# Relation passes of a graph network: messages and mixed rows worked on in PSUM, rings of four, squares of shares made by ScalarE

## The chip, the cores and the metric

The kernel runs on one core of a Trainium2 chip. The metric is the device time of one execution in microseconds. The names of the engines in the profile: PE is TensorE (PEld its weight loads), DVE is VectorE, ACT is ScalarE, POOL is GpSimd, SP is SyncE, which here only issues DMAs.

## The reference

Four graph layers run one after the other on x, 50000 nodes of 128 float32 values: a graph attention network, a relation network, a GraphSAGE network and an equivariant network, each added to x and normalized. The change touches only the relation network. It takes its input x as h, with 25000 edges (src, dst, type), dst sorted, and runs three cells:

```python
def _cell(h_in, relv, W, b, src, dst, rel, n_nodes):
    msg = jax.nn.relu(h_in[src] + relv[rel])
    s = jax.ops.segment_sum(msg, dst, num_segments=n_nodes)
    cnt = jax.ops.segment_sum(jnp.ones((src.shape[0],), msg.dtype), dst, num_segments=n_nodes)
    red = s / jnp.maximum(cnt, 1.0)[:, None]
    return red @ W.T + b
h = _cell(h, relvecs[0], lin_w[0], lin_b[0], ...)
for l in range(1, N_LAYERS):
    h_prev = h
    _h = jax.nn.relu(_layer_norm(h, ln_w[l - 1], ln_b[l - 1]))
    h = h_prev + _cell(_h, relvecs[l], lin_w[l], lin_b[l], ...)
h = _layer_norm(h, ln_w[-1], ln_b[-1])
```

After it, x becomes the layer norm of x + h. Only nodes with incoming edges differ from a closed form, so the kernel works on "slots", one per edge position in sorted order: 49 blocks of 512 slots (128 partitions, KT = 4 columns).

## The kernel before, in words

The program is a row of passes, each closed by a barrier of all engines. The three relation passes are `RelSlots(l)` for l = 0, 1, 2 (from 2728 us of the span to 3737). Before them lie the attention passes, behind them three sage passes (`SageSlots`) and the last pass `tp`.

Each engine runs its own list of steps through `times` (L136): a step has a lag, and at time t a step with lag d works on block t - d; the order inside the list is the order of issue within one time. Waits are on semaphores that count blocks: `done(engine, sem, b, back)` waits until block b - back has passed `sem`, `landed` waits for a DMA.

For one block b, in passes 0 and 1:

- GpSimd (L1687) issues four indirect DMAs, each of which fetches 128 rows of the sources into `G` (ring of 4). It waits for the messages of block g - 4. The descriptors of these DMAs are made on GpSimd itself.
- TensorE `messages` (L1702): one matmul adds the relation vectors (`relv` by a one-hot `oh`) into the bank `pt`, then four matmuls multiply each 128 gathered rows by a diagonal square with the shares (1 / count) of their slots, `kn.shares`. The result is turned: features on partitions, slots along the free dimension.
- ScalarE `relu` (L1741) writes it to SBUF as `mT` (ring of 2).
- VectorE `run_sums` (`run_scan`, L1603) scans along the slots with the 0/1 marks `kn.same`, which gives the segment sums `agT` (SBUF).
- TensorE `product` (L1715) multiplies by the weights into the bank `pw` (ring of 2).
- VectorE `mix` (L1794) adds the bias or the row of the cell before (`prev`) and writes `y` in SBUF. `next_bias` (L1805) adds the next bias for the store `yb`.
- ScalarE `square` (L1746) and `deviation` make the row norms' deviation. VectorE `scale` takes the reciprocal, `norm` (L1815) writes y * r * weight to `u` (SBUF), `cut` (L1822) does the relu against the negative bias. SP stores `yb` and `u`.

In pass 0 VectorE also makes the diagonal squares with the shares for all later passes (`spread_shares`, L1789: one 128x512 product of the identity with four columns of `shareD` spread out, both in SBUF).

Pass 2 has, in place of `next_bias`, `norm` and `cut`, the steps of `end_steps` (L1062): `gamma` (four scalings of y), `add_x` (adds the node's x, loaded to `xx`), `stats`, `aggregate`, `scale2`, `shift` on VectorE, `norm` on ScalarE (four activations to `nrm`). Then TensorE `turn` transposes `nrm` into the bank `pn` (L1724), ScalarE `keep_turned` (L1763) copies it to `nT` (ring of 2), SP stores it to `sage_slots_t` with lag 11 (L1671), TensorE `rows` multiplies it into the bank `pr` (L1729), ScalarE `keep_rows` (L1770) copies it to `res` (ring of 2), and SP stores that. `keep_turned` waits until the store of the block two before has landed.

Of the kernel before, what the change touches and what calls it, by code (L numbers as in the profile page):

```python
# [1608 lines left out]
class RelSlots(Stream):  # L1609


    def __init__(self, kn, q, l):
        self.kn, self.l, self.last = kn, l, l == 2
        self.G = q.sb("G", [P, 4, KT, D])
        self.Y = 2 if self.last else 4
        self.oh = q.sb("oh", [8, self.Y, BLOCK])
        self.mT = q.sb("mT", [P, 2, BLOCK])
        self.agT = q.sb("agT", [P, self.Y, BLOCK])
        self.y = q.sb("y", [P, self.Y, KT, D])
        self.yb = q.sb("yb", [P, 4, KT, D]) if l < 2 else None  # L1620
        self.prev = q.sb("prev", [P, 4, KT, D]) if l else None
        self.junk = q.sb("junk", [P, KT, D])
        self.ss, self.sd, self.rr = (q.sb(n, [P, 4, KT]) for n in ("ss", "sd", "rr"))
        self.pt = [q.ps(f"t{j}") for j in range(2)]
        self.pw = [q.ps(f"w{j}") for j in range(2)]
        self.gin, self.ohin, self.pin = (q.sems(n, 4) for n in ("rows_in", "kinds_in", "before_in"))
        if l < 2:
            self.stored, self.ystored = q.sems("stored", 4), q.sems("y_stored", 4)
        (self.mtm, self.mtk, self.scn, self.wm, self.shd, self.yn, self.ym, self.sq, self.sdm, self.rrd) = (
            q.sem(n) for n in ("messages_made", "messages_kept", "summed", "product_made", "shares_ready", "next_bias_added", "mixed",  # L1630
                               "squares_made", "deviation_ready", "scale_ready"))
        if self.last:
# [3 lines left out]
            self.e = kn.end_steps(self.parts, lambda b, k: self.y[:, b.m % self.Y, k, :], self.rr, self.ym, self.rrd, lambda n: kn.slot_at(kn.n0, kn.NP, n), None,  # L1636
                                  kn.lw[:, 2, :])
            self.nT = q.sb("nT", [P, 2, BLOCK])
            self.res = q.sb("res", [P, 2, KT, D])
            self.pn, self.pr = q.ps("nt"), q.ps("r")  # L1640
            self.tstored, self.rstored = q.sems("turned_stored", 4), q.sems("rows_stored", 4)
            self.gate, self.xb, self.ntr, self.ntk, self.rm, self.rk = (
                q.sem(n) for n in ("store_gate", "x_beta", "out_turned", "out_kept", "rows_made", "rows_kept"))
        else:
            self.u = q.sb("u", [P, 4, KT, D])
            self.un, self.um = q.sem("normed"), q.sem("result_ready")

    def sync(self, sp):
# [50 lines left out]
    def tensor(self, pe):  # L1699
        kn, l = self.kn, self.l  # L1700

        def messages(b):  # L1702
            landed(pe, self.ohin, b)
            landed(pe, self.gin, b, 0, 16 * KT)
            done(pe, self.mtk, b, 2)
            if l == 0:
                done(pe, self.shd, b)
            pt = self.pt[b.s2]
# [6 lines left out]
        def product(b):  # L1715
            done(pe, self.scn, b)
            done(pe, self.ym, b, 2)
            for k in range(KT):
                mm = pe.matmul(self.pw[b.s2][:, k * P:(k + 1) * P], self.agT[:, b.m % self.Y, k * P:(k + 1) * P], kn.Wr[:, l, :], start=True, stop=True)
            mm.then_inc(self.wm, 1)  # L1720
# [8 lines left out]
        def rows(b):  # L1729
            done(pe, self.ntk, b)  # L1730
            done(pe, self.rk, b, 1)
            for k in range(KT):
                mm = pe.matmul(self.pr[:, k * P:(k + 1) * P], self.nT[:, b.s2, k * P:(k + 1) * P], kn.Wn[:, 0, :], start=True, stop=True)
# [4 lines left out]
    def scalar(self, act):  # L1738
        kn, l = self.kn, self.l

        def relu(b):  # L1741
            done(act, self.mtm, b)
            done(act, self.scn, b, 2)
            act.activation(self.mT[:, b.s2, :], self.pt[b.s2][:, :], ACT.Relu).then_inc(self.mtk, 1)  # L1744

        def square(b):  # L1746
# [3 lines left out]
            for k in range(KT):  # L1750
                last = act.activation(self.junk[:, k, :], self.y[:, b.m % self.Y, k, :], ACT.Square, scale=D ** -0.5, accum_out=self.ss[:, b.s4, k:k + 1])
# [11 lines left out]
        def keep_turned(b):  # L1763
            done(act, self.ntr, b)
            done(act, self.rm, b, 2)
            if not isinstance(b.n, int) or b.n >= 2:
                act.wait_ge(self.tstored[(b.m + 2) % 4], (b.i + (b.m - 2) // 4 + 1) * 16)
            act.activation(self.nT[:, b.s2, :], self.pn[:, :], ACT.Copy).then_inc(self.ntk, 1)

        def keep_rows(b):  # L1770
            done(act, self.rm, b)
            if not isinstance(b.n, int) or b.n >= 2:
                act.wait_ge(self.rstored[(b.m + 2) % 4], (b.i + (b.m - 2) // 4 + 1) * 16)
            act.activation(self.res[:, b.s2].rearrange("p k d -> p (k d)"), self.pr[:, :], ACT.Copy).then_inc(self.rk, 1)
# [3 lines left out]
        return [(deviation, 5), (square, 4), (relu, 1)]  # L1778

    def vector(self, v):  # L1780
        kn, l = self.kn, self.l

        def run_sums(b):
# [55 lines left out]
        return ([] if l else [(spread_shares, 0)]) + [(cut, 6), (mix, 4), (run_sums, 2), (next_bias, 4), (scale, 5), (norm, 5)]  # L1839
# [1273 lines left out]
```

## Time and profile before

| | us |
|---|---|
| median of 3 runs | 5241.16 (5229.94 to 5247.69) |
| the profiled execution's own time | 5236.16 |
| its span | 5234.4 |
| PE / DVE / ACT / POOL busy | 3823.6 / 3793.3 / 3176.2 / 2889.9 |
| TensorE's granted clock, mean | 0.85 |
| relation pass 0, 1, 2 | 2728 to 3047, to 3348, to 3737 |

The busy time of an engine is an average over passes with different limits, so the rows of one pass say more than the table. A granted clock of 1.0 is 2.4 GHz and 0.5 is 1.2 GHz; a mean in between is a mix of the two. "Idle before" of a group is the time its engine waited just before its instructions, with what ended the wait; "issue" is idle time that ends with nothing the profile shows.

### The profile page before, as it was taken

Reading aid. Unit: us, or ns where it says so; the run is one execution under the profiler, and the core shown is the slowest. Engines: PE = TensorE matmul, PEld = TensorE weight load, DVE = VectorE, ACT = ScalarE, POOL = GpSimd, SP = SyncE. Lnnn points to the kernel's source line nnn. Section 1 sums busy time; section 2 is a strip of 40 time slices with the busy share of each in tenths; the row PEclk is TensorE's granted clock in tenths of the full one; section 3 lists DMA queues with packets and bytes.
Section 4 is the critical chain, followed back from the end, with each engine's and each line's share of the span. In section 5 each row is a group of like instructions: output and inputs, shape, how many; then the busy total and the mean of one; then the engine's idle time right before and its main releaser. Section 6 shows DMA issues by size and latency. Waiting matters only on the chain. (4 is left out here: it accounts for less than half of the span.)

```text
span 5234.4 us, 104308 instructions
## 1 busy us (share of the span) xinstructions
PE 3823.6 (73%) x23663; PEld 3147.4 (60%) x23663; DVE 3793.3 (72%) x10843; ACT 3176.2 (61%) x11279; POOL 2889.9 (55%) x2759
## 2 busy tenths in 40 slices
PE   6355889876877676577767767677688887967775
PEld 5254778765557455555655545466576676856665
DVE  1575889987869787887977767677577675746665
ACT  2022879786868687787753323366687685645554
POOL 0474767604730770175017767666374765757776
PEclk8698999988989898899766666688899998978777
DMA  8899999756965885598653446455598896772221
GB/s 183 117 295 276 378 371 294 248 149 188 286 202 155 238 280 170 158 281 263 169 165 119 131 147 188 153 180 185 187 307 284 271 305 224 245 173 58 64 67 55
DMA packets 918272, 1074.23 MB, mean 205 GB/s; under 512 B 202779, under 2 KB 565065, under 8 KB 917106
## 3 DMA queue, kind: packets, MB, share of 16 engines
q1 hardware_dynamic: 763570, 890.24, 52.2%
q0 software_dynamic: 90944, 180.06, 14.2%
q10 hardware_dynamic: 63556, 1.81, 1.7%
q14 instruction: 146, 1.20, 0.1%
q8 instruction: 56, 0.92, 0.1%
HBM read 509.54 MB, written 566.14 MB: 206 GB/s over the span
## 5 line engine op out<-in xcount | busy, mean ns | idle before, releaser
L2359 POOL DMA_INDIRECT H<-gat_rows,src_i x784 | 803.2, 1024 | 879.8 <-POOLq L80 641.8
L1910 POOL DMA_INDIRECT s_G<-sage_rows,src_i x588 | 604.1, 1027 | 363.5 <-issue 162.5
L1696 POOL DMA_INDIRECT r_G<-rel_rows,idx x392 | 438.4, 1118 | 207.9 <-issue 111.9
L2548 PE MATMUL p_M<-Wg,p_hT 128*128 128x132 f32 x2352 | 337.8, 287 | 64.2 <-DVE p_res L2605 49.5
L1709 PE MATMUL r_t<-r_oh,relv 8*128 8x512 f32 x294 | 227.1, 861 | 207.9 <-issue 94.6
L1744 ACT ACTIVATE r_mT<-r_t 128x512 f32<-128x512 f32 x147 | 87.3, 594 | 457.4 <-PE r_t L1712 457.3
L2548 PEld LDWEIGHTS p_M<-Wg,p_hT 128*128 128x128 f32 x2352 | 290.9, 192 | 115.2 <-issue 98.2
L2605 DVE SCALAR_TENSOR_TENSOR p_res<-p_M,p_rr,cg 128x132 f32<-128x132 f32 x1176 | 334.0, 346 | 2.3 <-PE p_M L2548 1.4
L1305 PE MATMUL d_S<-ones,d_sqT 128*128 128x1 f32 x1568 | 228.6, 267 | 135.9 <-DVE d_ve L1450 135.9
L2687 PEld LDWEIGHTS p_pl_p<-Wn,p_pl_h 128*128 128x128 f32 x1568 | 204.2, 197 | 205.3 <-ACT p_pl_h L2781 156.3
L2687 PE MATMUL p_pl_p<-Wn,p_pl_h 128*128 128x128 f32 x1568 | 223.7, 288 | 136.1 <-ACT p_pl_h L2781 134.2
L1305 PEld LDWEIGHTS d_S<-ones,d_sqT 128*128 128x128 f32 x1568 | 222.0, 218 | 162.7 <-issue 131.7
L1606 DVE TENSOR_TENSOR_SCAN r_agT<-same_run,r_agT,r_mT 128x512 f32<-128x512 f32 (+1 forms) x144 | 184.5, 1281 | 179.7 <-ACT r_mT L1744 179.7
L1712 PEld LDWEIGHTS r_t<-share_squares,r_G 128*128 128x128 f32 x1176 | 198.9, 256 | 159.5 <-issue 159.5
L1696 POOL DMA_INDIRECT r_G<-n_rows,src_i x196 | 235.8, 1203 | 78.5 <-issue 55.5
L2407 POOL DMA_INDIRECT H<-gat_rows,dst_i x196 | 196.1, 1001 | 141.1 <-POOLq L80 59.2
L2120 POOL DMA_INDIRECT share_squares<-features,src_i x196 | 217.1, 1108 | 93.0 <-issue 59.2
L964 POOL DMA_INDIRECT gat_rows<-early_mapv,early_mput x196 | 193.9, 989 | 122.7 <-PEq L77 59.6
L1354 ACT ACTIVATE d_hs<-d_hs,pl 128x128 f32<-128x128 f32 x784 | 248.3, 398 | 15.4 <-DMA d_hs<-gat_rows 11.6
L1444 DVE TENSOR_TENSOR_SCAN d_yT<-same_run,d_yT,d_T 128x512 f32<-128x512 f32 (+1 forms) x192 | 244.4, 1273 | 0.5 <-PE d_T L1298 0.4
L2112 POOL DMA_INDIRECT out_dram<-tp_v,put_i x196 | 198.1, 1011 | 78.8 <-issue 57.0
L1712 PE MATMUL r_t<-share_squares,r_G 128*128 (+1 forms) x1176 | 234.5, 361 | 0.0
(482 smaller groups left out, 12290.6 us busy)
## 6 DMA issues: line engine op xcount, KB each, us to landing
gat_rows<-p_res SPq DMA_DIRECT2D x294, 264.0 KB
sage_rows<-p_pl_s SPq DMA_DIRECT2D x294, 256.0 KB
gat_rows<-x_row SPq DMA_DIRECT2D x98, 536.0 KB
gat_rows<-d_res SPq DMA_DIRECT2D x147, 264.0 KB
d_hs<-gat_rows SPq DMA_DIRECT2D x147, 256.0 KB
s_hT<-sage_slots_t SPq DMA_DIRECT2D x147, 256.0 KB
slot_rows<-H SPq DMA_DIRECT2D x49, 544.0 KB, 11.3
x_x<-in_x SPq DMA_DIRECT2D x98, 256.0 KB
```

The source lines that it names most:

```text
L1305: mm = pe.matmul(pS[:, k:k + 1], sqT[:, b.s2, k * P:(k + 1) * P], self.ones[:, :], start=True, stop=True)
L1354: last = act.activation(hs[:, b.s4, k, :], hs[:, b.s4, k, :], ACT.Copy, scale=self.pl[:, bass.ds(b.n * KT + k, 1)])
L1444: v.tensor_tensor_scan(yT[:, b.s4, :], self.same[:, bass.ds(b.n * BLOCK, BLOCK)], pT[b.s2][:, :], 0.0 if first else yT[:, (b.m - 1) % 4, B ...
L1696: pool.indirect_dma_start(self.G[:, g % 4, k, :], None, table, bass.IndirectOffsetOnAxis(index[:, c:c + 1], 0), bounds_check=bound, oob_is ...
L1709: pe.matmul(pt[:, :], kn.relv[:, l, :], self.oh[:, b.m % self.Y, :], start=True, stop=False)
L1712: mm = pe.matmul(pt[:, k * P:(k + 1) * P], self.G[:, b.s4, k, :], share, start=False, stop=(k == KT - 1))
L1910: pool.indirect_dma_start(self.G[:, g % 4, k, :], None, kn.st[self.l], bass.IndirectOffsetOnAxis(kn.idx[:, c:c + 1], 0), bounds_check=boun ...
L2120: pool.indirect_dma_start(self.G[:, c, :], None, kn.f, bass.IndirectOffsetOnAxis(kn.idx[:, c:c + 1], 0), bounds_check=bound, oob_is_err=Fa ...
L2359: pool.indirect_dma_start(kn.H[:, c, 0:width], None, table, bass.IndirectOffsetOnAxis(index[:, c:c + 1], 0), bounds_check=bound, oob_is_er ...
L2548: mm = pe.matmul(self.pM[self.bank(b, j)][:, k // 2, (k % 2) * TW:(k % 2 + 1) * TW], self.hT[l][:, b.s2, k * P:(k + 1) * P], kn.Wg[:, l, : ...
L2605: last = v.scalar_tensor_tensor(self.res[l][:, b.s4, k, :], self.pM[self.bank(b, j)][:, k // 2, (k % 2) * TW:(k % 2 + 1) * TW], self.rr[l] ...
L2687: mm = pe.matmul(bank[:, k * D:(k + 1) * D], xT[:, k * P:(k + 1) * P], w, start=True, stop=True)
```

## The change

`mT` and `y` go. `relu` works in place in the message bank `pt`, and the scan reads it there. `mix` works in place in the product bank `pw`; `square`, `next_bias`, `norm` and `gamma` read it there, `norm` works in place, and `cut` brings its result from PSUM to `u` in SBUF. `pt` is a ring of four in passes 0 and 1 (two in pass 2), `pw` a ring of four in all, so all eight banks are in use. In pass 2 `nT` and `res` become rings of four. In pass 0 VectorE only copies four columns of shares (`pick_shares`), and ScalarE makes the four diagonal squares from the identity with a scale per partition (`spread_shares`).

```diff
-        self.mT = q.sb("mT", [P, 2, BLOCK])
-        self.y = q.sb("y", [P, self.Y, KT, D])
-        self.pt = [q.ps(f"t{j}") for j in range(2)]
-        self.pw = [q.ps(f"w{j}") for j in range(2)]
+        self.pt = [q.ps(f"t{j}") for j in range(2 if self.last else 4)]
+        self.pw = [q.ps(f"w{j}") for j in range(4)]
-            self.nT = q.sb("nT", [P, 2, BLOCK])
-            self.res = q.sb("res", [P, 2, KT, D])
+            self.nT = q.sb("nT", [P, 4, BLOCK])
+            self.res = q.sb("res", [P, 4, KT, D])
+        if not l:
+            self.column, self.picked = q.sb("column", [P, 4, KT]), q.sem("shares_picked")
 # messages (TensorE)
-            done(pe, self.mtk, b, 2)
+            done(pe, self.scn, b, len(self.pt))
 # product (TensorE)
-            done(pe, self.ym, b, 2)
+            done(pe, self.gr if self.last else self.um, b, 4)
 # ScalarE
+        def spread_shares(b):
+            done(act, self.picked, b)
+            for k in range(KT):
+                square = kn.shares[:, bass.ds(b.n * KT + k, 1), :].rearrange("p o n -> p (o n)")
+                last = act.activation(square, kn.ident[:, :], ACT.Copy, scale=self.column[:, b.s4, k:k + 1])
+            last.then_inc(self.shd, 1)
+
         def relu(b):
             done(act, self.mtm, b)
-            done(act, self.scn, b, 2)
-            act.activation(self.mT[:, b.s2, :], self.pt[b.s2][:, :], ACT.Relu).then_inc(self.mtk, 1)
+            pt = self.pt[b.m % len(self.pt)]
+            act.activation(pt[:, :], pt[:, :], ACT.Relu).then_inc(self.mtk, 1)
 # keep_turned; keep_rows likewise
-            done(act, self.rm, b, 2)
-            if not isinstance(b.n, int) or b.n >= 2:
-                act.wait_ge(self.tstored[(b.m + 2) % 4], (b.i + (b.m - 2) // 4 + 1) * 16)
+            done(act, self.rm, b, 4)
+            landed(act, self.tstored, b, 4)
+        return ([] if l else [(spread_shares, 0)]) + [(deviation, 5), (square, 4), (relu, 1)]
 # VectorE
-        def spread_shares(b):
-            c = bass.ds(b.n * KT, KT)
-            v.tensor_tensor(kn.shares[:, c, :], spread(kn.ident[:, :], KT), fan(kn.shareD[:, c], P), ALU.mult).then_inc(self.shd, 1)
+        def pick_shares(b):
+            done(v, self.shd, b, 4)
+            v.tensor_copy(self.column[:, b.s4, :], kn.shareD[:, bass.ds(b.n * KT, KT)]).then_inc(self.picked, 1)
 # mix
-            done(v, self.sq, b, self.Y)
-            done(v, self.gr if self.last else self.un, b, self.Y)
-                v.tensor_tensor(self.y[:, b.m % self.Y].rearrange("p k d -> p (k d)"), self.pw[b.s2][:, :], before, ALU.add).then_inc(self.ym, 1)
+                v.tensor_tensor(pw[:, :], pw[:, :], before, ALU.add).then_inc(self.ym, 1)
 # next_bias
-            done(v, self.ym, b)
+            done(v, self.sq, b)
 # norm
-            landed(v, self.stored, b, 4)
-            for k in range(KT):
-                last = v.scalar_tensor_tensor(self.u[:, b.s4, k, :], self.y[:, b.m % self.Y, k, :], self.rr[:, b.s4, k:k + 1], kn.lw[:, l, :], ALU.mult, ALU.mult)
+            done(v, self.yn, b)
+            for k in range(KT):
+                y = self.pw[b.s4][:, k * P:(k + 1) * P]
+                last = v.scalar_tensor_tensor(y, y, self.rr[:, b.s4, k:k + 1], kn.lw[:, l, :], ALU.mult, ALU.mult)
 # cut
-            v.tensor_tensor(self.u[:, b.s4], self.u[:, b.s4], spread(kn.nbb[:, l, :], KT), ALU.max).then_inc(self.um, 1)
+            landed(v, self.stored, b, 4)
+            v.tensor_tensor(self.u[:, b.s4], self.pw[b.s4][:, :].rearrange("p (k d) -> p k d", k=KT), spread(kn.nbb[:, l, :], KT), ALU.max).then_inc(self.um, 1)
-        return ([] if l else [(spread_shares, 0)]) + [(cut, 6), (mix, 4), (run_sums, 2), (next_bias, 4), (scale, 5), (norm, 5)]
+        return ([] if l else [(pick_shares, 0)]) + [(cut, 6), (mix, 4), (run_sums, 2), (next_bias, 5), (scale, 5), (norm, 5)]
```

## Rows read from the trace of the kernel before

**Rows 1.** The page's chain that ended last, shares of the span by line.

```profile
POOL out_dram L2112 3%; POOL share_squares L2120 3%; PE tp_w L2165 1%; PE tp_u L2149 0%; DMA tp_records<-records 0%; PE tp_h L2142 0%; PE tp_t L2157 0%; ACT tp_U L2191 0%; DVE tp_agT L1606 0%; DVE tp_v L2268 0%; ACT tp_ws L2193 0%; DVE tp_v L2278 0%; ACT tp_lT L2180 0%; DMA out_dram<-tp_v,put_i 0%; DVE tp_t L2228 0%
```

**Rows 2.** Windows by pass: us; PE, PEld, DVE, ACT, POOL busy; clock, DMA, GB/s.

```profile
2728.00:3047.00 319.00, 234.31 (x882) 163.65 (x882) 239.49 (x490) 97.67 (x490) 235.81 (x196) 0.67 0.39 124
3047.00:3348.00 301.00, 217.32 (x882) 153.78 (x882) 213.28 (x441) 98.41 (x490) 218.64 (x196) 0.69 0.57 174
3348.00:3737.00 389.00, 285.99 (x1470) 223.04 (x1470) 272.32 (x931) 230.45 (x833) 219.80 (x197) 0.79 0.52 168
```

**Rows 3.** GpSimd in passes 0, 1, 2: busy, mean ns | idle before, releasers.

```profile
L1696 POOL DMA_INDIRECT r_G<-n_rows,src_i x196 | 235.8, 1203 | 78.5 <-issue 55.5 <-POOLq L80 19.1 <-PE r_t L1712 4.0
...
L1696 POOL DMA_INDIRECT r_G<-rel_rows,idx x196 | 218.6, 1116 | 83.0 <-issue 59.1 <-POOLq L80 23.6 <-PE r_t L1712 0.3
...
L1696 POOL DMA_INDIRECT r_G<-rel_rows,idx x196 | 219.8, 1121 | 124.9 <-issue 52.7 <-PE r_t L1712 49.9 <-POOLq L80 22.2
```

**Rows 4.** The same view over all sage passes.

```profile
L1910 POOL DMA_INDIRECT s_G<-sage_rows,src_i x588 | 604.1, 1027 | 363.5 <-issue 162.5 <-POOLq L80 152.4 <-PE s_t L1921 48.6
```

**Rows 5.** Timeline of pass 0: start, us, engine line op names.

```profile
2861.85 1.28 DVE L1606 TENSOR_TENSOR_SCAN r_agT<-same_run,r_agT,r_mT 128x512 f32<-128x512 f32 x1 [1.29 <-ACT r_mT L1744]
...
2862.44 1.50 POOL L1696 DMA_INDIRECT r_G<-n_rows,src_i  x1 [0.30 <-issue]
...
2865.50 0.69 DVE L1824 TENSOR_TENSOR r_u<-r_u,nbb 128x512 f32<-128x512 f32 x1
2865.63 1.43 POOL L1696 DMA_INDIRECT r_G<-n_rows,src_i  x1 [0.30 <-issue]
```

**Rows 6.** Timeline of a sage pass.

```profile
4202.16 1.27 DVE L1606 TENSOR_TENSOR_SCAN s_agT<-same_run,s_agT,s_t 128x512 f32<-128x512 f32 x1
...
4202.67 1.00 POOL L1910 DMA_INDIRECT s_G<-sage_rows,src_i  x1 [0.30 <-issue]
...
4203.54 0.69 DVE L3026 TENSOR_TENSOR s_pe_o<-s_pe_base,s_pe_rro 128x512 f32<-128x512 f32 x1
...
4203.97 1.14 POOL L1910 DMA_INDIRECT s_G<-sage_rows,src_i  x1 [0.30 <-issue]
```

**Rows 7.** Waits in pass 2: who <- whom, us in total, times, longest.

```profile
ACT r_nT L1768 <- DMA sage_slots_t<-r_nT: 84.9, 33, 4.9
PE r_nt L1726 <- ACT r_nrm L1138: 63.6, 27, 4.5
POOL r_G L1696 <- PE r_t L1712: 49.9, 22, 5.3
```

**Rows 8.** Instructions on the tile r_agT: ns min/median/max, first and last start.

```profile
L1606 DVE TENSOR_TENSOR_SCAN r_agT<-same_run,r_agT,r_mT x144: 1252/1283/1348, 2746.7 to 3693.4; 128x512 f32<-128x512 f32 x112, 128x512 f32<-128x512 uint8 x32
L1606 DVE TENSOR_TENSOR_SCAN r_agT<-same_run,r_mT x3: 1224/1224/1225, 2741.5 to 3360.1; 128x512 f32<-128x512 uint8 x3
```

**Rows 9.** Groups of VectorE by shape: scans from PSUM (s_t), SBUF (r_mT).

```profile
L1606 DVE TENSOR_TENSOR_SCAN s_agT<-same_run,s_agT,s_t 128x512 f32<-128x512 f32 x120 | 153.2, 1276 | 5.4 <-issue 2.0
L1606 DVE TENSOR_TENSOR_SCAN r_agT<-same_run,r_agT,r_mT 128x512 f32<-128x512 f32 x112 | 143.5, 1281 | 131.2 <-ACT r_mT L1744 131.2
```

**Rows 10.** Groups: scaled activation of ScalarE; smallest operation of VectorE in pass 0.

```profile
L1354 ACT ACTIVATE d_hs<-d_hs,pl 128x128 f32<-128x128 f32 x784 | 248.3, 398 | 15.4 <-DMA d_hs<-gat_rows 11.6 <-DMA d_hs<-slot_rows 3.8
...
L1813 DVE RECIPROCAL r_rr<-r_sd 128x4 f32<-128x4 f32 x49 | 8.4, 170 | 0.0
```

**Rows 11.** A window late in pass 2, columns as in Rows 2.

```profile
3620.00:3694.00 74.00, 56.53 (x342) 43.98 (x342) 61.43 (x211) 52.83 (x195) 32.84 (x31) 0.93 0.63 212
```

**Rows 12.** Timeline of pass 2, start and drain: TensorE at low clock.

```profile
3377.99 2.04 PE L1709 MATMUL r_t<-r_oh,relv 8*128 8x512 f32 x2 [1.69 <-issue]
...
3379.95 2.08 PE L1712 MATMUL r_t<-share_squares,r_G 128*128 128x128 f32 x8
...
3702.38 1.11 PE L1726 MATMUL r_nt<-ident,r_nrm 128*128 128x128 f32 x4 [4.02 <-ACT r_nrm L1138]
...
3703.28 1.92 PE L1733 MATMUL r_r<-Wn,r_nT 128*128 128x128 f32 x8
```

More of the change, by code:

```diff
@@ L1716, in product @@
             done(pe, self.scn, b)
-            done(pe, self.ym, b, 2)
+            done(pe, self.gr if self.last else self.um, b, 4)
             for k in range(KT):
-                mm = pe.matmul(self.pw[b.s2][:, k * P:(k + 1) * P], self.agT[:, b.m % self.Y, k * P:(k + 1) * P], kn.Wr[:, l, :], start=True, stop=True)
+                mm = pe.matmul(self.pw[b.s4][:, k * P:(k + 1) * P], self.agT[:, b.m % self.Y, k * P:(k + 1) * P], kn.Wr[:, l, :], start=True, stop=True)
             mm.then_inc(self.wm, 1)
@@ L1732, in rows @@
             for k in range(KT):
-                mm = pe.matmul(self.pr[:, k * P:(k + 1) * P], self.nT[:, b.s2, k * P:(k + 1) * P], kn.Wn[:, 0, :], start=True, stop=True)
+                mm = pe.matmul(self.pr[:, k * P:(k + 1) * P], self.nT[:, b.s4, k * P:(k + 1) * P], kn.Wn[:, 0, :], start=True, stop=True)
             mm.then_inc(self.rm, 1)
@@ L1739, in scalar @@
         kn, l = self.kn, self.l
+        def spread_shares(b):
[4 more added lines that the diff above has]
+            last.then_inc(self.shd, 1)
         def relu(b):
             done(act, self.mtm, b)
-            done(act, self.scn, b, 2)
-            act.activation(self.mT[:, b.s2, :], self.pt[b.s2][:, :], ACT.Relu).then_inc(self.mtk, 1)
+            pt = self.pt[b.m % len(self.pt)]
+            act.activation(pt[:, :], pt[:, :], ACT.Relu).then_inc(self.mtk, 1)
         def square(b):
@@ L1750, in square @@
             for k in range(KT):
-                last = act.activation(self.junk[:, k, :], self.y[:, b.m % self.Y, k, :], ACT.Square, scale=D ** -0.5, accum_out=self.ss[:, b.s4, k:k + 1])
+                last = act.activation(self.junk[:, k, :], self.pw[b.s4][:, k * P:(k + 1) * P], ACT.Square, scale=D ** -0.5, accum_out=self.ss[:, b.s4, k:k + 1])
             last.then_inc(self.sq, 1)
@@ L1764, in keep_turned @@
             done(act, self.ntr, b)
-            done(act, self.rm, b, 2)
-            if not isinstance(b.n, int) or b.n >= 2:
-                act.wait_ge(self.tstored[(b.m + 2) % 4], (b.i + (b.m - 2) // 4 + 1) * 16)
-            act.activation(self.nT[:, b.s2, :], self.pn[:, :], ACT.Copy).then_inc(self.ntk, 1)
+            done(act, self.rm, b, 4)
+            landed(act, self.tstored, b, 4)
+            act.activation(self.nT[:, b.s4, :], self.pn[:, :], ACT.Copy).then_inc(self.ntk, 1)
         def keep_rows(b):
             done(act, self.rm, b)
-            if not isinstance(b.n, int) or b.n >= 2:
-                act.wait_ge(self.rstored[(b.m + 2) % 4], (b.i + (b.m - 2) // 4 + 1) * 16)
-            act.activation(self.res[:, b.s2].rearrange("p k d -> p (k d)"), self.pr[:, :], ACT.Copy).then_inc(self.rk, 1)
+            landed(act, self.rstored, b, 4)
+            act.activation(self.res[:, b.s4].rearrange("p k d -> p (k d)"), self.pr[:, :], ACT.Copy).then_inc(self.rk, 1)
         if self.last:
             return [(deviation, 5), (self.e["deviation2"](act), 7), (keep_turned, 9), (square, 4), (keep_rows, 10), (norm, 8), (relu, 1)]
-        return [(deviation, 5), (square, 4), (relu, 1)]
+        return ([] if l else [(spread_shares, 0)]) + [(deviation, 5), (square, 4), (relu, 1)]
     def vector(self, v):
```

15 lines of the change are left out of this document (8 added, 7 removed).

## The prediction

> **What bounds the kernel now.** I read the chain of waits first. It names only the last pass of the program: the passes are closed by barriers, so no long chain runs back into the relation passes [rows 1]. What a change there is worth has to be read pass by pass, from the stretch of each one: 319, 301 and 389 us [rows 2]. The groups of GpSimd's instructions come next. Each relation pass gathers 49 blocks with 4 indirect DMAs each, and in passes 0 and 1 GpSimd does nothing else: 235.8 us busy, 55.5 us of issue (about 0.28 us behind each gather) and only 4.0 us of waiting for TensorE, 295.3 us in all; in pass 1 218.6 + 59.1 + 0.3 = 278.0 us [rows 3]. The rest of both passes is fill and drain. So passes 0 and 1 are bound by the issue of gathers.
>
> The mean gather is 1203 ns in pass 0, 1116 and 1121 ns in passes 1 and 2, and 1027 ns over the 588 gathers of the sage passes, which do the same work [rows 3, 4]. The timeline says why. In pass 0 the gather at 2862.44 begins while a scan runs whose two tensor inputs lie in SBUF, and takes 1.50 us; the one at 2865.63 begins under `cut`, also with two SBUF inputs, and takes 1.43 [rows 5]. In a sage pass the gather at 4202.67 begins equally far into a scan (0.51 us after its start, against 0.59) and takes 1.00. That scan reads its rows from PSUM. A little later one that starts under an operation with two SBUF inputs (`s_pe_base`, `s_pe_rro`) takes 1.14 [rows 6]. So a VectorE operation with two SBUF inputs holds a gather up by up to about 0.5 us, and one with a PSUM input does not.
>
> The Trainium skill, "SBUF — State Buffer", section "SBUF: two separate sides", has VectorE and GpSimd share a port pair that a VectorE operation with two SBUF inputs takes against a GpSimd operation that reads SBUF; the two gathers under scans agree. Its section "Who interferes with whom" infers that such a tensor_tensor should not stall the making of descriptors. By that nothing would be won here; the 1.43 us gather under `cut` speaks against it.
>
> Pass 2 is different. There GpSimd waits 49.9 us for TensorE, ScalarE waits 84.9 us, in 33 of 49 blocks, to overwrite a turned block (`r_nT`, ring of two) until its store has landed, and TensorE waits 63.6 us for `r_nrm`, which stands behind that wait on ScalarE [rows 7]. From the first scan at 3360.1 to the last at 3693.4 are 48 periods of 6.94 us [rows 8].
>
> **The change, part by part.**
>
> Messages and mixed rows in PSUM, passes 0 and 1. The scan, `next_bias`, `norm` and `cut` each get one input from PSUM in place of SBUF; `mix` had one already. Their count and sizes stay. The gathers' excess over 1.00 us is 196 x 0.203 = 39.8 us in pass 0 and 196 x 0.116 = 22.7 us in pass 1. No operation of these passes with two large SBUF inputs remains, so all but a few us should go: I take -38 and -21 (the sage passes, which keep one or two such operations, still show 0.027 us each, 5 us for 196) [rows 3, 4].
>
> What is late next: at 1.30 us a gather a block takes 5.2 us. VectorE's work in pass 0 is 239.5 / 49 = 4.9 us a block, 4.2 without `spread_shares`; pass 1's is 213.3 / 49 = 4.4. ScalarE's is 2.0. TensorE's is 4.8 and 4.4 at a granted clock of 0.67 and 0.69, so it has room, and more whenever the clock is high [rows 2]. All stay below 5.2. Two rings of four banks each let TensorE run further ahead; nothing waits on them today, so that is worth 0.
>
> Price of PSUM operands on VectorE. The scan takes 1276 ns from PSUM and 1281 from SBUF [rows 9]. So reading costs 0, within 5 ns either way. No row shows VectorE or ScalarE writing PSUM. I bound it from below by the same 5 ns and from above, far off, by one more of the smallest operation of the pass, 0.17 us, per write [rows 10]: 5 writes a block (`mix`, four `norm`) are 0.85 us, which 4.2 and 4.4 a block still hold within about 5.2; pass 2 has only `mix`, 8 us. I take 0, by the row of the scan, which is nearest.
>
> The Trainium skill speaks against the change here: "Perfetto Trace Analysis", section "Optimizing Scalar/DVE Operations", gives VectorE about 65 ns more per instruction on PSUM than on SBUF. An estimate by that page for pass 2, with its five instructions a block that move to PSUM sources (scan and four `gamma`), is 49 x 5 x 0.065 = 16 us less gain. The two scans just named do not show it.
>
> Squares with the shares by ScalarE, pass 0. VectorE loses 49 operations and gains 49 copies of 4 columns (the smallest operation of the pass takes 0.17). ScalarE gets 196 scaled 128x128 activations; the nearest row has 784 of them in 248.3 us busy, 0.32 each, so 62 us, on an engine that is busy 97.7 of 319 [rows 2, 10]. Its mean of one, 0.40, would make 78. Either lies beside ScalarE's waits. Queued behind `spread_shares` on ScalarE are `deviation`, `square` and `relu` of older blocks; the new wait is for VectorE's 4-column copy. From one `relu` over scan, `next_bias`, `norm`, copy, squares, `square` to the `relu` two blocks on is 1.3 + 0.7 + 0.2 + 1.1 + 0.2 + 1.3 + 0.3 + 1.3 + 0.6 = 7.0 us (the scan by its row, the squares 4 x 0.32, the others rounded from the same timeline) for two blocks, against 10.4 that the gathers take: hidden, 0. The squares are written a block before TensorE reads them.
>
> Waits that are new on VectorE: `next_bias` for the squares of `square`, one block later than it stood before, and `norm` for `next_bias`, which is two instructions earlier. Both are over by then: 0.
>
> Pass 2, rings of four. The store of a turned block is issued two steps after it is kept; now ScalarE needs it back four blocks later, not two, some 12 us instead of 6. The whole wait of 84.9 us goes, and the next resource ends the period. VectorE: 272.3 / 49 = 5.56 us a block. Gathers: 5.2 plus what `add_x` and `x_beta` (still two SBUF inputs) hold up, of today's 0.12 x 4 = 0.5 about half. TensorE: 286.0 / 49 = 5.84 at clock 0.79, 4.6 were it always at the full one. ScalarE: 4.7 [rows 2]. So VectorE, at 5.6 plus small gaps. Where the clock was 0.93 the engines already came near: VectorE 61.4 of 74 us [rows 11]. I take 6.05 for the mean, between 5.6 and today's 6.94, since some low-clock stretches will stay: 48 x 0.89 = -43. The drain (39 us behind the last scan, one bank each for turned and rows) stays. Rings of four for `res` and `pw`: their waits are in no row, 0. The DMAs are as many as before.
>
> Sum: -38 - 21 - 43 = -102 against the profiled execution's 5236.2, so 5134; the median shown is 5241.2, by which it is 5139. I write 5136.
>
> **Rivals.**
>
> B, pass 2 stays: the store wait goes but low-clock stretches or the load of `r_xx` hold the period at 6.8 to 6.9. For: TensorE needs 5.84 on average already. Gain 59 and a few us: 5175.
>
> C, the change doesn't free the gathers: PSUM operations hold them as well, or writing PSUM does. Only pass 2 gains: 5236 - 43 = 5193. Against: the 1.00 us gather under a scan from PSUM [rows 6]. This is also the case of the page's second section.
>
> D, better than forecast: dense work keeps TensorE's clock up and pass 2 runs at VectorE's 5.65: 48 x 1.29 = -62, sum -121: 5115.
>
> E, slower: TensorE falls to the lower of its levels (1.2 GHz) for all of pass 2. A block is then 1.11 (turn) + 1.92 (rows) + 2.04 + 2.08 (messages) + 1.92 (product) = 9.1 us [rows 12]. That is 48 x 2.1 = +103 in pass 2 against -59 in the others: 5280. It decides from a mean period of 8.2 us on. For: the spaced-out drain ran at that level. Against: with the wait gone TensorE has shorter gaps than now, and at 0.93 where the periods were short [rows 11].
>
> **How the numbers follow.** Forecast 60%, B 20%, C 6%, D 10%, E 4%. The likeliest case alone spans 5120 to 5152 (pass 2 at 5.75 to 6.4). The range leaves out E, the far side of D and half of C: 5112 to 5186. A difference under 0.3% (16 us) can't be told from no change here. Faster by more: all but E and a small part in which B and C meet with dear PSUM writes: 0.92. Within: 0.04, slower: 0.04.
>
> **What would show it.** Mean gather 1.00 to 1.03 us in passes 0 and 1, 1.05 to 1.08 in pass 2; GpSimd's first to last gather 257 us in pass 0 and 1; no wait of `r_nT` for its store; scans of pass 2 every 6.0 us; the scan still 1.28 and `mix` 0.68. Wrong if gathers in passes 0 and 1 stay at 1.1 or more, if GpSimd there waits for TensorE for over 15 us, or if pass 2 keeps 6.8.

## The result and the profile after

The changed kernel takes 5102.5 us (median of 4 runs, 5099.1 to 5105.3) against 5238.6 for the kernel before beside it: ratio 0.973, 95% interval 0.971 to 0.975. The profiled execution took 5105.3 us, its span is 5103.5 us (5234.4 before), its mean clock 0.862 (0.850).

The windows of the three relation passes, and inside pass 2 a stretch of its steady part: length; PE, PEld, DVE, ACT, POOL busy; granted clock, DMA share, GB/s. They answer to [rows 2].

```profile
2724.00:3002.00 278.00, 214.54 (x882) 152.93 (x882) 215.02 (x490) 147.20 (x686) 195.71 (x196) 0.71 0.45 142
3002.00:3281.00 279.00, 211.15 (x882) 150.70 (x882) 212.46 (x441) 91.96 (x490) 195.63 (x196) 0.71 0.61 187
3281.00:3607.00 326.00, 256.29 (x1470) 194.51 (x1470) 264.20 (x931) 224.77 (x833) 209.35 (x197) 0.88 0.62 200
3360.00:3500.00 140.00, 118.98 (x758) 90.36 (x757) 134.65 (x478) 114.38 (x431) 109.44 (x101) 1.00 0.73 238
```

The gathers of passes 0, 1 and 2, grouped: busy, mean ns of one | idle time before them and its causes. They answer to [rows 3].

```profile
L1696 POOL DMA_INDIRECT r_G<-n_rows,src_i x196 | 195.7, 999 | 79.7 <-issue 57.6 <-POOLq L80 20.2 <-PE r_t L1712 1.8
...
L1696 POOL DMA_INDIRECT r_G<-rel_rows,idx x196 | 195.6, 998 | 82.9 <-issue 58.2 <-POOLq L80 23.4 <-PE r_t L1712 1.2
...
L1696 POOL DMA_INDIRECT r_G<-rel_rows,idx x196 | 209.2, 1067 | 83.7 <-issue 59.1 <-POOLq L80 24.2 <-PE r_t L1712 0.3
```

The first to the last gather, as busy + issue + TensorE wait: 255.1 us in pass 0 (295.3 before), 255.0 in pass 1 (278.0), 268.6 in pass 2 (322.4). The mean gather fell from 1203 and 1116 to 999 and 998 ns; in pass 2 from 1121 to 1067, and its wait of 49.9 us for TensorE is gone.

The instructions on `r_agT`, for [rows 8], and the waits between 3300 and 3560 us, for [rows 7] (us in total, times, longest):

```profile
L1606 DVE TENSOR_TENSOR_SCAN r_agT<-same_run,r_agT,r_t x144: 1247/1270/1281, 2742.0 to 3565.1; 128x512 f32<-128x512 f32 x112, 128x512 f32<-128x512 uint8 x32
L1606 DVE TENSOR_TENSOR_SCAN r_agT<-same_run,r_t x3: 1220/1220/1221, 2736.8 to 3294.6; 128x512 f32<-128x512 uint8 x3
```

```profile
ACT r_sd L1114 <- DVE r_mv L1106: 43.9, 41, 2.7
...
PE r_nt L1726 <- ACT r_nrm L1138: 31.0, 37, 1.0
```

Pass 2's scans now run from 3294.6 to 3565.1: 48 periods of 5.64 us, 270.5 in all against 333.3. The wait of `r_nT` for its store has no row any more. The one for `r_nrm` has halved, from 63.6 to 31.0 us, and none of its parts is over 1.0.

The sum over the span: pass 0 -40.2, pass 1 -23.0, pass 2's scans -62.8, together -126.0 of -130.9 in the span. Of the rest 4.3 us lie ahead of the first gather, in work that the change doesn't touch; that start came at 2720.9 to 2726.2 us in the four programs tried on one chip, which are alike up to there.

### The profile page after: what moved, and what is told of

Its sections match the earlier page's. It is cut to its first block and busy times, and to the rows that moved or that the text cites. A ratio compares the mean times of both kernels' runs of the same rounds, so it can differ in the third digit from the quotient of the medians.

```text
span 5103.5 us, 104447 instructions
## 1 busy us (share of the span) xinstructions
PE 3761.0 (74%) x23663; PEld 3105.7 (61%) x23663; DVE 3758.0 (74%) x10843; ACT 3214.3 (63%) x11475; POOL 2811.2 (55%) x2759
## 5 line engine op out<-in xcount | busy, mean ns | idle before, releaser
L1696 POOL DMA_INDIRECT r_G<-rel_rows,idx x392 | 404.8, 1033 | 166.5 <-issue 117.4
L1709 PE MATMUL r_t<-r_oh,relv 8*128 8x512 f32 x294 | 205.3, 784 | 171.2 <-DMA r_G<-rel_rows,idx 72.8
L1751 ACT ACTIVATE r_t<-r_t 128x512 f32<-128x512 f32 x147 | 86.7, 590 | 324.3 <-PE r_t L1712 324.1
L1712 PEld LDWEIGHTS r_t<-share_squares,r_G 128*128 128x128 f32 x1176 | 187.4, 242 | 143.8 <-issue 143.8
L1606 DVE TENSOR_TENSOR_SCAN r_agT<-same_run,r_agT,r_t 128x512 f32<-128x512 f32 (+1 forms) x144 | 182.5, 1268 | 105.0 <-ACT r_t L1751 104.6
L1027 ACT ACTIVATE x_xT<-x_T 128x512 f32<-128x512 f32 x98 | 58.5, 597 | 289.6 <-PE x_T L1010 289.6
L1696 POOL DMA_INDIRECT r_G<-n_rows,src_i x196 | 195.7, 999 | 79.7 <-issue 57.6
```

The lines of the kernel that those rows point to most:

```text
L1696: pool.indirect_dma_start(self.G[:, g % 4, k, :], None, table, bass.IndirectOffsetOnAxis(index[:, c:c + 1], 0), bounds_check=bound, oob_is ...
L1709: pe.matmul(pt[:, :], kn.relv[:, l, :], self.oh[:, b.m % self.Y, :], start=True, stop=False)
```

## The experiments

Two pairs of rivals were tested. For passes 0 and 1: VectorE operations with two SBUF inputs hold gathers up, against PSUM banks and looser waits let the pipeline run. For pass 2: the store waits were the cost, against the gathers' hold or the banks. Four kernels ran on a chip where the kernel before takes 5236 us: the two with one ring at two, the unedited one beside them, and the last of all. The other eight ran on chips where it takes 5219 and 5221. So times are compared by ratio or inside a pass.

**Rings of two again.** The changed kernel, both rings of pass 2 as before:

```
-            self.nT = q.sb("nT", [P, 4, BLOCK])
-            self.res = q.sb("res", [P, 4, KT, D])
+            self.nT = q.sb("nT", [P, 2, BLOCK])
+            self.res = q.sb("res", [P, 2, KT, D])
...
-            landed(act, self.tstored, b, 4)
+            if not isinstance(b.n, int) or b.n >= 2:
+                act.wait_ge(self.tstored[(b.m + 2) % 4], (b.i + (b.m - 2) // 4 + 1) * 16)
```

> The changed kernel with nT and res back as rings of two in pass 2 (everything else kept). Theory (the store wait was the stall of pass 2): ScalarE waits again for the store of the turned block, 50 to 85 us in sum, TensorE's clock in pass 2 falls from 0.88 to about 0.8, scans come every 6.5 to 6.9 us instead of 5.6, and the kernel takes 45 to 60 us more than the changed one (5150 to 5165). Passes 0 and 1 stay at 278 us each. Rival (pass 2 gained because the rows lie in PSUM and the gathers are free): the wait stays small, scans at 5.6 to 5.9, the kernel within 15 us of 5102.

5149.0 us, ratio 0.987 (0.984 to 0.989). Passes 0 and 1 keep 254.9 and 254.8 us. Its waits in pass 2 and its scans:

```profile
ACT r_nT L1775 <- DMA sage_slots_t<-r_nT: 87.3, 32, 4.6
POOL r_G L1696 <- PE r_t L1712: 66.7, 24, 5.9
```

```profile
L1606 DVE TENSOR_TENSOR_SCAN r_agT<-same_run,r_agT,r_t x144: 1246/1279/1282, 2719.7 to 3603.5; 128x512 f32<-128x512 f32 x112, 128x512 f32<-128x512 uint8 x32
L1606 DVE TENSOR_TENSOR_SCAN r_agT<-same_run,r_t x3: 1220/1221/1221, 2714.5 to 3270.5; 128x512 f32<-128x512 uint8 x3
```

The period is 333.0 / 48 = 6.94 again, as before the change. Pass 2's scans take 62.5 us more than the 270.5 of the changed kernel, a little over the 45 to 60 expected. So all that pass 2 won depends on the rings: with rings of two, PSUM gives it nothing.

**Each ring by itself.** The same edit for `res` alone, and for `nT` alone.

> The changed kernel with the ring of result rows (r_res) at two and the ring of the turned rows (r_nT) at four. Against the earlier version that had the same two rings, but its mixed rows in SBUF (period 6.30 us, end of pass 2 at 352 us after its first gather), it differs by the mixed rows in PSUM alone. Theory (the result rows' store is the next wait: it held ACT 41.8 us in that version): period 6.1 to 6.4, ACT waits 30 to 50 us for the store of r_res, 25 to 35 us slower than the changed kernel. Rival (mixed rows in PSUM and four product banks made the rest): period 5.6 to 5.8, under 8 us slower than the changed kernel.

> The changed kernel with the ring of the turned rows (r_nT) at two and the ring of result rows (r_res) at four. Theory (each ring of two holds ACT by itself; the turned rows' store first): period 6.5 to 6.95, ACT waits 75 to 90 us for the store of r_nT, 45 to 65 us slower than the changed kernel, nearly all of what both rings of two cost together. Rival (the two rings share the cost evenly): period 6.2 to 6.4, 25 to 40 us slower.

With `res` at two 5128.4 us, ratio 0.980 (0.978 to 0.982); with `nT` at two 5158.0, ratio 0.985 (0.983 to 0.987); the unedited kernel in the same call 5103.4, ratio 0.974 (0.972 to 0.976). First the waits of pass 2 with `res` at two, then those with `nT` at two and its window:

```profile
ACT r_res L1780 <- DMA sage_rows<-r_res: 47.4, 34, 3.2
```

```profile
ACT r_nT L1775 <- DMA sage_slots_t<-r_nT: 85.7, 35, 4.5
...
3276.00:3652.00 376.00, 281.37 (x1470) 218.93 (x1470) 268.97 (x931) 224.31 (x833) 198.75 (x196) 0.80 0.53 173
```

The scans of pass 2 take 289.7 us (3292.6 to 3582.3, 6.04 each) with `res` at two, 324.1 (3287.7 to 3611.8, 6.75 each) with `nT` at two, 268.7 unedited: +21.0 and +55.4. Both rivals fell. The theory for `nT` held in full; `res` costs a little less than was expected of it, 6.04 a period against 6.1 to 6.4 and 25.0 us in the whole time against 25 to 35. The costs don't add (together 62.5): the longer wait hides most of the shorter. With `nT` at two the clock over the pass is 0.80, near the 0.79 of [rows 2]; with `res` at two it is 0.87, near the 0.88 of the changed kernel.

> The changed kernel, unedited, beside the others of this call on the same chip: ratio 0.972 to 0.975 to the kernel before; the gathers of pass 2 over 268 to 270 us. It is the base for the differences of a few us that the other runs show.

This base came out as written, gathers of pass 2 over 269.5 us.

**Messages in PSUM alone.** The kernel before; `relu` in place in PSUM, the scan reads it, the message banks are four in passes 0 and 1 as in the change; `y`, the product banks and the rings of pass 2 stay:

```
-            act.activation(self.mT[:, b.s2, :], self.pt[b.s2][:, :], ACT.Relu).then_inc(self.mtk, 1)
+            act.activation(pt[:, :], pt[:, :], ACT.Relu).then_inc(self.mtk, 1)
```

> The kernel before with the messages alone in PSUM (relu in place, message banks as in the change; y, mix, next_bias, norm, cut, the squares by VectorE and the rings of two as before). So of the operations with two SBUF inputs only the scan changes. Theory (each operation with two SBUF inputs holds the gathers): part of the gathers' excess goes, mean gather in pass 1 from 1116 to about 1060 (next_bias, norm, cut remain), in pass 0 from 1203 to 1110 to 1150; passes 0 and 1 together 20 to 35 us shorter. Pass 2 keeps its wait for the store and its length (within 8 us). Rival (all of the excess is the scan's, the longest): gathers at 1000 to 1020 in pass 1.

5207.9 us, ratio 0.998 (0.996 to 1.000). From the first gather to the last, pass 0 is 291.6 us, pass 1 270.7: only -3.7 and -7.3, where 20 to 35 together were expected. This is the expectation that failed most. Its gathers of pass 0, and its timeline there (start, duration):

```profile
L1695 POOL DMA_INDIRECT r_G<-n_rows,src_i x196 | 232.1, 1184 | 78.3 <-issue 55.8 <-POOLq L80 18.9 <-PE r_t L1711 3.7
```

```profile
2858.82 0.69 DVE L1790 TENSOR_TENSOR share_squares<-ident,shareD 128x512 f32 x1
...
2859.05 1.93 POOL L1695 DMA_INDIRECT r_G<-n_rows,src_i  x1 [0.30 <-issue]
...
2859.42 0.69 DVE L1823 TENSOR_TENSOR r_u<-r_u,nbb 128x512 f32<-128x512 f32 x1
```

The scan holds nothing now: 46 gathers of pass 0 begin under one, all of usual length. But the gathers come sooner and the next one begins under the squares, with `cut` right behind: 1.93 us in place of 1.00. Its excess of 0.93 is the time from its start to the end of `cut` (2860.11), 1.06, less 0.13. Under the squares begin 33 gathers of pass 0, late by 0.83 us in the mean; in the kernel before it was one. VectorE's row of operations follows the gathers' data, so the two stay in step (argued, not tested), and whichever operation with two SBUF inputs stands where a gather begins takes the hold over. Most of the gain comes with the last of them: the four kinds left in pass 0 (squares, `norm`, `cut`, `next_bias`) keep 36 of 40 us, the squares alone, below, 9.

**The same with the turned ring at four.** `nT` of four, `res` of two, mixed rows in SBUF.

```
-            self.nT = q.sb("nT", [P, 2, BLOCK])
+            self.nT = q.sb("nT", [P, 4, BLOCK])
```

> The previous kernel with a ring of four for nT alone (SBUF has room for it only because mT is gone; res stays at two, and y in SBUF). Theory (the wait for the store of the turned block is the whole stall of pass 2): the wait goes, TensorE's clock in pass 2 rises to 0.86 or more, scans come every 5.6 to 5.8 us, pass 2 gets 50 to 62 us shorter than in the previous kernel. Rival (mixed rows in PSUM and the ring of four product banks give a good part): only 20 to 40 us.

5172.3 us, ratio 0.991 (0.989 to 0.993). Its scans of pass 2 run from 3333.1 to 3635.7, 6.30 each, and the next store takes over:

```profile
ACT r_res L1772 <- DMA sage_rows<-r_res: 41.8, 28, 2.9
```

They take 302.6 us, 33.2 less than the 335.8 (3322.2 to 3658.0) of the version without the ring; 50 to 62 were expected. The changed kernel with the same two rings has 6.04: mixed rows in PSUM, with four product banks, are worth 12.9 us in pass 2 there. Four in both rings was not tried on the kernel before, since it doesn't fit beside `mT` and `y`: by the tiles' shapes the two longer rings need 8192 bytes more of each partition, and `mT` and `y` hold 8192 in pass 2. That space is the other thing that the move to PSUM brought.

**Squares by VectorE again**, the changed kernel otherwise:

```
-        return ([] if l else [(spread_shares, 0)]) + [(deviation, 5), (square, 4), (relu, 1)]
+        return [(deviation, 5), (square, 4), (relu, 1)]
...
-            done(v, self.shd, b, 4)
-            v.tensor_copy(self.column[:, b.s4, :], kn.shareD[:, bass.ds(b.n * KT, KT)]).then_inc(self.picked, 1)
+            c = bass.ds(b.n * KT, KT)
+            v.tensor_tensor(kn.shares[:, c, :], spread(kn.ident[:, :], KT), fan(kn.shareD[:, c], P), ALU.mult).then_inc(self.shd, 1)
```

> The changed kernel with the diagonal squares of the shares made by VectorE again in pass 0, one 128x512 operation with two SBUF inputs a block. Theory (an operation with two SBUF inputs holds back the gather that starts under it): mean gather in pass 0 goes from 999 ns to 1040 to 1090, pass 0 and the kernel get 8 to 18 us longer (5110 to 5120); passes 1 and 2 unchanged. Rival (the squares' place matters by the engines' load only): VectorE then has 4.9 us a block, under 5.2, so gathers stay at 1000 ns and the time within 3 us.

5084.1 us, ratio 0.974 (0.972 to 0.976), and pass 0:

```profile
L1696 POOL DMA_INDIRECT r_G<-n_rows,src_i x196 | 204.8, 1045 | 78.6 <-issue 57.6 <-POOLq L80 19.1 <-PE r_t L1712 1.8
```

204.8 + 57.6 + 1.8 = 264.2 us, 9 more than 255.1, in the range expected; passes 1 and 2 are unchanged. ScalarE's share of the change is worth 9 us, too little to tell in the whole time.

**Message banks of two in all passes.**

```
-        self.pt = [q.ps(f"t{j}") for j in range(2 if self.last else 4)]
+        self.pt = [q.ps(f"t{j}") for j in range(2)]
```

> The changed kernel with two message banks in passes 0 and 1 instead of four (the messages of a block then wait for the scan of the block two before). Theory (rings of four banks for messages are worth nothing while gathers are the bound): time within 5 us of the changed kernel, gathers back to back in both passes. Rival (TensorE running further ahead is part of the gain): GpSimd waits for TensorE 10 us or more per pass and the kernel takes 15 to 30 us longer.

5077.6 us, ratio 0.974 (0.972 to 0.976); gathers 254.7, 254.6 and 269.2 us. Four message banks are worth nothing.

**One more VectorE operation in pass 1**, 128x512, into a tile of its own that nothing reads; first with two SBUF inputs, then with one of them in PSUM:

```
+            v.tensor_tensor(self.extra[:, :, :], spread(kn.ident[:, :], KT), spread(kn.br[:, 0, :], KT), ALU.add).then_inc(self.xt, 1)
...
+            v.tensor_tensor(self.extra[:, :, :], self.pw[b.s4][:, :].rearrange("p (k d) -> p k d", k=KT), spread(kn.br[:, 0, :], KT), ALU.add).then_inc(self.xt, 1)
```

> The changed kernel with one more VectorE operation a block in pass 1, 128x512, both inputs in SBUF, its result unused. VectorE's load rises to about 5.0 us a block, under the 5.2 of the gathers. Theory (port): mean gather in pass 1 from 998 to 1040 to 1100 and the pass 8 to 18 us longer. Rival (load alone counts): the same length as the next kernel.

> As the last kernel, but the first input of the extra operation is the product bank in PSUM: same size, same place, same waits. Theory (port): mean gather in pass 1 stays at 998 to 1003 and the pass within 3 us of the changed kernel's 255 us from first to last gather. Rival: as long as the kernel with two SBUF inputs.

5090.5 us, ratio 0.975 (0.973 to 0.976), and 5080.0, ratio 0.974 (0.972 to 0.975). The gathers of pass 1, first kernel and second:

```profile
L1698 POOL DMA_INDIRECT r_G<-rel_rows,idx x196 | 199.4, 1017 | 82.2 <-issue 58.3 <-POOLq L80 22.7 <-PE r_t L1714 1.2
```

```profile
L1698 POOL DMA_INDIRECT r_G<-rel_rows,idx x196 | 195.2, 996 | 82.6 <-issue 58.2 <-POOLq L80 23.2 <-PE r_t L1714 1.2
```

The place of the inputs makes the difference, 4.2 us, with operations of 693 and 691 ns and the same waits. The size fell short of the 8 to 18 expected. The timeline of the first kernel says why:

```profile
3099.43 0.69 DVE L1820 TENSOR_TENSOR r_extra<-ident,br 128x512 f32<-128x512 f32 x1
...
3099.72 1.27 POOL L1698 DMA_INDIRECT r_G<-rel_rows,idx  x1 [0.30 <-issue]
...
3105.20 1.00 POOL L1698 DMA_INDIRECT r_G<-rel_rows,idx  x1 [0.30 <-issue]
...
3105.31 0.69 DVE L1820 TENSOR_TENSOR r_extra<-ident,br 128x512 f32<-128x512 f32 x1
```

The operation that runs when the gather begins ends 0.40 us later, and the gather is 0.27 too long: 0.40 less 0.13. The one that starts 0.11 us into a gather does nothing to it, and takes its usual 0.69 us itself. Only 21 of the 49 ran at a gather's start, and 12 of these held it; in the second kernel 22 ran at one and none held it.

**Pass 2 without two SBUF inputs.** `gamma` in place in PSUM, beta added there, the x rows last; `product` waits for that last sum, and the sum with beta (`x_beta`) moves up to the second place in VectorE's order:

```
-            done(pe, self.gr if self.last else self.um, b, 4)
+            done(pe, self.parts[3] if self.last else self.um, b, 4)
...
+                last = v.scalar_tensor_tensor(y, y, self.rr[:, b.s4, k:k + 1], kn.lw[:, 2, :], ALU.mult, ALU.mult)
...
-            v.tensor_tensor(xx, xx, spread(kn.bb2[:, :], KT), ALU.add).then_inc(self.xb, 1)
+            v.tensor_tensor(rows, rows, spread(kn.bb2[:, :], KT), ALU.add).then_inc(self.xb, 1)
...
-            self.e["add_x"](v)(b)
+            v.tensor_tensor(e["v"][:, b.s4], rows, e["xx"][:, b.s4], ALU.add).then_inc(self.parts[3], 1)
```

> The changed kernel with the last two large two-SBUF-input operations of pass 2 turned to one SBUF input: gamma works in place in the product bank, the beta is added there, and add_x adds the loaded x to it while writing v. Same count and sizes of operations. Theory: mean gather in pass 2 goes from 1067 ns to 1000 to 1010, gathers would allow a block every 5.2 us, and VectorE (264 us for 49 blocks, 5.4) is the bound: scans every 5.4 to 5.5 instead of 5.55 to 5.6, 4 to 10 us less, 5092 to 5098. Rival (the gathers are not what sets pass 2): gathers get shorter but the period stays and so does the time, within 3 us.

5081.4 us, ratio 0.975 (0.972 to 0.977). The gathers are free (996 ns), and the period is 5.70, longer than the 5.60 unedited, where 5.4 to 5.5 was expected. From its waits over 150 us of pass 2:

```profile
PEld r_w L1719 <- DVE r_v L1851: 19.6, 21, 1.0
```

TensorE's `product` now waits for `add_x` of four blocks before, which VectorE reaches late: the hold was traded for a wait.

**The same with `add_x` ahead of the scan**, which then covers that wait; `x_beta` goes last.

```
-            return [..., (mix, 4), (e["scale2"](v), 8), (run_sums, 2), (e["shift"](v), 8), (add_x, 6), ...]
+            return [(e["aggregate"](v), 7), (mix, 4), (e["scale2"](v), 8), (add_x, 6), (run_sums, 2), (e["shift"](v), 8), (scale, 5),
+                    (gamma, 5), (e["stats"](v), 6), (x_beta, 5)]
```

> The changed kernel with the norm's weights, beta and the x rows of pass 2 all applied to the product's bank in PSUM (as in the version with no input pair in SBUF), and with VectorE's order set so that the sum with the x rows comes ahead of the scan, which then covers TensorE's wait for the bank. Theory (what is left in pass 2 is GpSimd at 5.57 us a block, of which the held gather is 0.31 to 0.35): scans of pass 2 at 5.4 to 5.5 us, 4 to 10 us faster than the changed kernel. Rival (VectorE's own work, 5.5 us a block, and its gaps bound pass 2 as much): gathers of 1.00 us with new waits, period 5.6 to 5.8, within 3 us of the changed kernel.

5093.6 us (5 runs, 5082.1 to 5105.4), ratio 0.972 (0.970 to 0.975), against 5103.4 for the changed kernel in the same call. Its steady window, gathers of passes 1 and 2, and scans:

```profile
3360.00:3500.00 140.00, 124.30 (x772) 92.05 (x771) 137.24 (x487) 119.47 (x438) 107.12 (x108) 1.00 0.76 248
```

```profile
L1696 POOL DMA_INDIRECT r_G<-rel_rows,idx x392 | 390.5, 996 | 168.7 <-issue 115.5 <-POOLq L80 49.9 <-PE r_t L1712 3.4
...
L1606 DVE TENSOR_TENSOR_SCAN r_agT<-same_run,r_agT,r_t x144: 1264/1272/1282, 2742.7 to 3558.5; 128x512 f32<-128x512 f32 x112, 128x512 f32<-128x512 uint8 x32
L1606 DVE TENSOR_TENSOR_SCAN r_agT<-same_run,r_t x3: 1220/1221/1221, 2737.4 to 3296.7; 128x512 f32<-128x512 uint8 x3
```

261.8 / 48 = 5.45 us a block, 6.9 us less over the pass than the unedited kernel's 268.7; the six profiles with pass 2 as in the change have 267.8 to 270.5. VectorE is busy 137.24 of 140 us, and pass 2's gathers are through in 254.7 us, ahead of the scans: now VectorE is the bound. The profile shows the gain in the pass; in the whole time the intervals overlap, so that this version beats the changed kernel is likely and not shown.

## Why the prediction was right or wrong

5136 us was forecast, 5112 to 5186, and 5102.5 measured. Between the two profiled executions it is -102 against -130.9: of the 28.9 us between, 19.8 are the period of pass 2, 4.2 passes 0 and 1, 4.3 lie ahead of the first gather, 0.6 elsewhere.

**Passes 0 and 1, the freed gathers: right.** -38 and -21 were forecast, -40.2 and -23.0 measured; 1.00 to 1.03 us a gather and 257 us from first to last against 999 and 998 ns and 255. Nothing took the hold's place: GpSimd waits 1.8 and 1.2 us for TensorE. The reason given, two SBUF inputs, is shown by the pair of added operations. It was incomplete: "a VectorE operation with two SBUF inputs holds a gather up by up to about 0.5 us" leaves out when. [Rows 5] had it: the scan ends at 2863.13, 0.69 us after the gather began, and the gather is 0.50 too long; `cut` ends 0.56 after, and the excess is 0.43. Counted over pass 0 of the kernel before, 138 of the 196 gathers begin under some VectorE operation, and these have the whole excess of 39.8 us; the other 58 have none. In the changed kernel 150 begin under one, 143 of these under an operation with an input in PSUM (scans and `norm` among them), 7 under a copy or reciprocal of four columns, and none is held.

The Trainium skill, "SBUF — State Buffer", has a shared port pair of VectorE and GpSimd in "SBUF: two separate sides", and the added operations agree: 1017 ns a gather with both inputs in SBUF, 996 with one. In "Who interferes with whom" it infers that a tensor_tensor leaves descriptor making alone; the gathers are held by one all the same. But a gather also reads its row numbers from SBUF, and no run tells whether that reading is held or the making of descriptors.

**The price of PSUM operands: right, 0.** `mix`, which now writes PSUM, takes 691 ns in pass 0 (684 before), `norm`, which reads and writes it, 353 (348), the scan 1275:

```profile
L1606 DVE TENSOR_TENSOR_SCAN r_agT<-same_run,r_agT,r_t 128x512 f32<-128x512 f32 (+1 forms) x48 | 61.2, 1275 | 46.0 <-ACT r_t L1751 45.9
L1825 DVE SCALAR_TENSOR_TENSOR r_w<-r_w,r_rr,lw 128x128 f32<-128x128 f32 x196 | 55.6, 353 | 1.7
...
L1808 DVE TENSOR_TENSOR r_w<-r_w,br 128x512 f32<-128x512 f32 x49 | 33.8, 691 | 0.0
```

The 65 ns per instruction that the Trainium skill's "Perfetto Trace Analysis", "Optimizing Scalar/DVE Operations", puts on PSUM do not show in any of the three.

**Squares by ScalarE: right.** 62 us forecast, and the group of pass 0 has it, beside 116 us in which ScalarE still waits for `relu`'s input:

```profile
L1745 ACT ACTIVATE share_squares<-ident,r_column 128x128 f32 (+1 forms) x196 | 62.0, 389 | 26.5 <-DVE r_column L1796 26.5
```

**Pass 2: the mechanism right, the term mis-sized.** -43 was forecast, -62.8 measured, which is rival D's -62. The step that failed is "I take 6.05 for the mean, between 5.6 and today's 6.94, since some low-clock stretches will stay". The mean is 5.64. One such stretch stayed, over the first 60 us of the scans, with periods up to 6.1 us; from 3355 us on the granted clock is 1.00 and the period 5.57. The two windows:

```profile
3295.00:3355.00 60.00, 54.87 (x230) 39.85 (x230) 41.99 (x127) 28.19 (x119) 46.22 (x46) 0.69 0.50 149
3355.00:3565.00 210.00, 177.54 (x1130) 134.97 (x1130) 201.93 (x720) 171.07 (x638) 153.95 (x142) 1.00 0.74 243
```

With `nT` at two put back the clock over the pass is 0.80. So the low clock went with the store wait. Wait and clock can be told apart in part, by stretches at a clock of 1.00 that have a store wait in them. Here is one of the kernel before, where the scans come every 6.49 us, and one of the version with `res` at two, where they come every 6.01:

```profile
3614.00:3640.00 26.00, 18.37 (x121) 14.10 (x122) 22.11 (x76) 18.58 (x69) 17.32 (x17) 1.00 0.63 206
```

```profile
3464.00:3560.00 96.00, 73.18 (x481) 56.11 (x480) 87.22 (x305) 73.58 (x273) 67.00 (x65) 1.00 0.68 224
```

So at the full clock the wait for `res` alone adds 0.44 us to 5.57, and the kernel before, which waits for `nT` and has its gathers held too, is 0.92 above it. From 3434 to 3586 us of the kernel before, at a clock of 0.72 to 0.79, the period is 7.5 to 7.7. Whether the clock lengthened those periods or the longer gaps lowered the clock, no run separates.

The wait itself was read too mildly: "some 12 us instead of 6". In the kernel before ScalarE is ready to overwrite a block 1.6 us after its store was issued (median), but a store takes 3.3 us to land, so ScalarE starts only 3.5 us after the issue. In the changed kernel it comes 12.9 us after. The whole wait went, as forecast.

The bound named for the new period was off as well. GpSimd is the full engine: 109.44 us busy and 101 gaps of 0.30 between gathers make 139.7 of 140, while VectorE has 134.65. That D's 5.65, worked out for VectorE, comes so near is in part luck. From the timeline of the changed kernel's pass 2:

```profile
3422.42 0.66 DVE L1836 TENSOR_TENSOR r_xx<-r_xx,bb 128x512 f32<-128x512 f32 x1
...
3422.56 1.39 POOL L1696 DMA_INDIRECT r_G<-rel_rows,idx  x1 [0.30 <-issue]
3424.26 1.00 POOL L1696 DMA_INDIRECT r_G<-rel_rows,idx  x1 [0.30 <-issue]
```

About one gather of four begins under `x_beta` (41 of the pass) and takes 1.37 to 1.39 here: 4 x 1.30 + 0.37 = 5.57 a block. VectorE's row lies so near that freeing GpSimd wins only 0.14 a block, 5.60 to 5.45. "Of today's 0.12 x 4 = 0.5 about half" gave 5.45 for the gathers, 0.12 too little.

**"Their waits are in no row, 0"** was said of the rings for `res` and `pw`. For `pw` no run changes the ring alone; with the mixed rows in PSUM it is worth 12.9 us. The 0 for four message banks holds. For `res` the 0 fails: once the wait for `nT` is gone, a `res` ring of two costs 21 us in pass 2 and ScalarE 47.4 us of waiting. The forecast credited the whole of the `nT` wait and took for granted that nothing would stand behind it; the change had covered that, not the argument.

**The rivals.** B fell with the period of 5.64, C with gathers of 999 ns, D is what came, with GpSimd as the bound in place of VectorE, E fell with a granted clock of 0.88 over the pass.

## What to carry to other kernels

Count, at the start of every GpSimd gather, which VectorE operation is running: if both its inputs are in SBUF the gather is late by about what is left of it. Taking one such operation away may only hand the hold to the next; most of the gain comes with the last. A wait that shows no row may only stand in another's shadow: when a ring is made longer, look for every store that the same engine waits for, and lengthen those rings together. A granted clock that is low in a stretch full of waits is not to be carried over into the forecast for the stretch without them.

## What was not expected of the hardware

The hold is sharp. In pass 0 of the kernel before a gather is too long by what is left of the operation at its start, less 0.19 us for a scan and 0.13 for a tensor_tensor or a scalar_tensor_tensor, to within 0.01 in nearly all of the 128 gathers held by over 0.06 us. Two such operations back to back hold one gather through both (1.93 us).

ScalarE reads PSUM faster and pays some back: `square` takes 267 ns and its read of the accumulator 200 in pass 0, against 297 and 189 from SBUF; in pass 2 281 and 213 against 298 and 190, which pays all of it back. The two groups of pass 0:

```profile
L1758 ACT ACTIVATE r_junk<-r_w 128x128 f32<-128x128 f32 x196 | 50.5, 267 | 5.3 <-DVE r_w L1808 5.3
L1758 ACT ACTIVATION_READ_ACCUMULATOR r_junk<-r_w 128x1 f32 x196 | 39.3, 200 | 0.0
```
